# Feed-forward on one core: FP4 codes turned as packed words, scales turned and spread by DMA, remainders on GpSimd

## What is computed

```
def fp4_quant_dequant(x):                 # blocks of 16 along the last dim
    scale = max(max|x| / 6, 1e-12)
    q = GRID[searchsorted(MID, |x / scale|)] * sign(x) * scale
    # GRID = 0, .5, 1, 1.5, 2, 3, 4, 6
def fp4_linear(x, w):
    return einsum('bsk,nk->bsn', fp4_quant_dequant(x), fp4_quant_dequant(w))

x = x + attention(layernorm(x))
n = layernorm(x)                          # eps 1e-5
h = silu(fp4_linear(n, w_gate)) * fp4_linear(n, w_up)      # 512 -> 1408
out = x + fp4_linear(h, w_down)                            # 1408 -> 512
```

## Time and profile before

| | us |
|---|---|
| median of 3 runs (lowest, highest) | 3051.26 (3050.97, 3052.3) |
| the profiled execution's own time | 3052.97 |
| its span | 3051.2 |
| TensorE busy | 2989.1 (98%) |
| VectorE busy | 2622.9 (86%) |
| ScalarE busy | 1350.4 (44%) |
| GpSimd busy | 755.0 (25%) |
| DMA queue, share of 16 engines | 35.8% |
| granted TensorE clock over the run | 0.993 |

### The profile page before, as it was taken

One profiled execution on the slowest core, in us unless ns is written; L12 is line 12 of the kernel. 1 busy time (PEld: TensorE's weight loads), 2 busy tenths in 40 slices (PEclk: granted clock), 3 DMA queues, 4 the chain that ended last, 5 costly groups with the idle time before them and its releaser, 6 DMA issues.

```text
span 3051.2 us, 65181 instructions
## 1 busy us (share of the span) xinstructions
PE 2989.1 (98%) x23204; PEld 2208.6 (72%) x23204; DVE 2622.9 (86%) x4209; ACT 1350.4 (44%) x2010; POOL 755.0 (25%) x680
## 2 busy tenths in 40 slices
PE   7999899999999999889999999999999999999999
PEld 6787644444444444478888888888888888888887
DVE  7999788889889888888888888888888888888886
ACT  5666577877777787532222222222222222222221
POOL 3444200000000000023333333333333333333332
PEclk9999899999999999999999999999999999999999
DMA  7889856655655665521111111111111111101110
GB/s 244 283 289 300 275 123 143 149 133 137 154 133 138 149 137 137 151 84 32 38 42 42 42 35 35 42 41 42 42 33 36 42 42 41 42 30 40 42 35 15
DMA packets 247628, 304.20 MB, mean 100 GB/s; under 512 B 21968, under 2 KB 154960, under 8 KB 247504
## 3 DMA queue, kind: packets, MB, share of 16 engines
q1 hardware_dynamic: 247504, 302.88, 35.8%
HBM read 190.35 MB, written 112.46 MB: 99 GB/s over the span
## 4 chain that ended last, share of the span: by engine, by line
PE 56%; DVE 1%; ACT 0%; DMA 0%; issue 0%; POOL 0%; SPq 0%; DVEq 0%
PE p_ring L1845 20%; PE p_ring L1873 16%; PE ps_od L1845 11%; PE ps_od L1825 5%; PE p_ring L1863 3%; PE p_ring L1853 1%; DVE sb_wg_lo L1751 0%; PE ps_od L1873 0%; PE p_ring L1825 0%; PE p_ring L1888 0%; DVE sb_fp_tmp L102 0%; DVE sb_wd_lo L1751 0%; DMA dn<-sb_fp_tmp 0%; DVE sb_h_amax L88 0%; DVE sb_stage L1722 0%
## 5 line engine op out<-in xcount | busy, mean ns | idle before, releaser
L1040 ACT ACTIVATE sb_probs<-scores 128x1024 f32<-128x1024 f32 (+3 forms) x512 | 405.8, 840 | 113.7 <-PE scores L1246 107.3
L788 POOL TENSOR_TENSOR sb_at_in<-sb_at_in,sb_inv_in 128x512 f32<-128x512 f32 x64 | 89.0, 1390 | 1069.0 <-DMA sb_inv_in<-dinv 1068.3
L1845 PE MATMUL p_ring<-sb_wg_hi,sb_xq_hi 128*128 128x512 f32 (+1 forms) x1024 | 295.2, 369 | 0.3 <-DVE sb_wd_lo L1751 0.3
L1548 POOL TENSOR_TENSOR sb_stage<-sb_stage,sb_h_inv 128x512 f32<-128x512 f32 (+1 forms) x192 | 210.8, 1098 | 339.2 <-DVE sb_h_inv L94 339.2
L1845 PE MATMUL p_ring<-sb_wg_lo,sb_xq_hi 128*128 128x512 f32 (+1 forms) x1024 | 290.5, 365 | 0.0
L1845 PE MATMUL p_ring<-sb_wg_hi,sb_xq_lo 128*128 128x512 f32 (+1 forms) x1024 | 289.9, 364 | 0.0
L1873 PE MATMUL p_ring<-sb_wd_hi,sb_ht_hi 128*128 128x512 f32 x693 | 275.9, 398 | 0.0
L1246 PEld LDWEIGHTS scores<-sb_q_hi,sb_k_hi 32*128 32x128 f32 x1536 | 73.7, 182 | 278.3 <-ACT sb_probs L1040 154.6
L1873 PE MATMUL p_ring<-sb_wd_hi,sb_ht_lo 128*128 128x512 f32 x693 | 270.2, 390 | 0.0
L1873 PE MATMUL p_ring<-sb_wd_lo,sb_ht_hi 128*128 128x512 f32 x693 | 269.8, 389 | 0.0
L1554 POOL TENSOR_TENSOR sb_stage<-sb_stage,sb_h_scale 128x512 f32<-128x512 f32 (+1 forms) x192 | 190.0, 989 | 267.4 <-DVE sb_stage L104 267.4
(11 more groups left out here) (203 smaller groups left out, 7172.3 us busy)
## 6 DMA issues: line engine op xcount, KB each, us to landing
kq<-sb_kq_out SPq DMA_DIRECT2D x32, 1024.0 KB, 7.2
sb_kq_raw<-kq SPq DMA_DIRECT2D x64, 512.0 KB, 6.8
sb_xin<-in_L_attn_x_dram SPq DMA_DIRECT2D x32, 512.0 KB, 6.9
v<-sb_v_out SPq DMA_DIRECT2D x64, 256.0 KB, 6.5
rq<-sb_r_out SPq DMA_DIRECT2D x64, 256.0 KB, 4.4
sb_qr<-rq SPq DMA_DIRECT2D x32, 512.0 KB
sb_kr_hi<-kr SPq DMA_DIRECT2D x32, 512.0 KB
sb_kr_lo<-kr SPq DMA_DIRECT2D x32, 512.0 KB
```

What stands on the lines that cost most here:

```text
L1040: act.activation(probs(k)[:, 2 * pair:2 * pair + 2, off:BANK], scores[(2 * k + pair) % RING2][:, :, off:BANK], ACT.Exp, scale=SCALE).then_ ...
L1548: pool.tensor_tensor(x, x, spread(h_inv[:, a // QB:b // QB], (b - a) // QB), ALU.mult).then_inc(h_y, 1)
L1845: i = pe.matmul(ps[:, m, 0:b0 - a0], xt[a][:, c, :], wg[b][:, m, c, a0:b0], start=(c == 0 and a == b == 0), stop=(c == DC - 1 and a == 1))
```

## The change

What TensorE turns is no longer the quantised float32 tile. After the two rounding steps ScalarE writes the value as an unsigned byte, code = value * 2^23 + 64, four features to a 32-bit word; one 128x128 transpose of words turns 512 features. VectorE decodes out of PSUM (`decode`: byte minus 64, times the turned scale) into SBUF. The block scales are turned by themselves: VectorE's 32x32 transpose of 128x32, a DMA to a scratch tensor in DRAM, and a DMA back that spreads each row over four partitions (for slice 2 three DMAs). The product with the scale before turning (L1711 and `hidden_q`) is gone. The normalisation of x moves from VectorE (L1697) to ScalarE (`normalise`), for which GpSimd makes a shift. Both `rest_of_x` and `rest_of_hidden` move from VectorE, where they read PSUM, to GpSimd, where they read SBUF. `x_in` is gone: x is loaded straight into `x1` by its own DMA. The silu result is written into h in place. The orders of all bodies are changed, `rest_of_attention` on GpSimd and the output store on SP among them. Weight columns are turned in the order c, c+4, c+8, ... so that the packing matches.

The diff, cut to its core ("..." marks what is left out):

```
+def fp4_half_scales(dve, x, amax, scale, inv, sem, base):
+    dve.tensor_reduce(amax, blocks_of(x), AX_X, ALU.max, apply_absolute_value=True).then_inc(sem, 1)
+    own(dve, sem, base + 1)
+    dve.tensor_scalar(scale, amax, SIXTH / 2, MIN_SCALE / 2, ALU.mult, ALU.max).then_inc(sem, 1)
...
 # SyncE
             def body(b, j):
                 q, r = b * HALF + j // UNROLL3, j % UNROLL3
+                if exists(q, r + 2):
+                    sp.wait_ge(stored[(r + 2) % 4], count(q, (r + 2) // 4 * 4, 4, 16))
+                    ahead.load_x(sp, b, j + 2)
                 if exists(q, r + 3):
                     sp.wait_ge(ps_free, number(q, r, "WO") + RING3 + 1)
                     ahead.load_tile(sp, b, j + 3)
-                if exists(q, r - 1):
-                    store(b, j - 1)
+                if exists(q, r + 1):
+                    store_x_scale(q, r + 1)
+                    spread_x_scale(q, r + 1)
+                for s in range(2):
+                    spread_h_scale(q, r, s)
                 if exists(q, r + 3):
                     sp.wait_ge(ahead.at_divided, count(q, r, 1, 3))
                     ahead.load_inverse(sp, b, j + 3)
+                spread_h_scale(q, r, 2)
+                if exists(q, r - 1):
+                    store(b, j - 1)
 # GpSimd
             def inverse_deviation(q, r):
+                pool.wait_ge(ln_steps, count(q, r, 3, 2))
+                pool.tensor_tensor(negmean[:], moments[:, 0:1], minus[:], ALU.mult).then_inc(s_rstd, 1)
                 pool.wait_ge(ln_steps, count(q, r, 3, 3))
                 pool.tensor_tensor(rstd[:], vareps[:], mhalf[:], ALU.pow).then_inc(s_rstd, 1)
+                own(pool, s_rstd, count(q, r, 3, 3))
+                pool.tensor_tensor(shift[:], negmean[:], rstd[:], ALU.mult).then_inc(s_rstd, 1)
+            def rest_of_x(q, r):
+                pool.wait_ge(x_hi, count(q, r, 1, 1))
+                pool.tensor_tensor(xt_lo[:], x_values, xt_hi[:].bitcast(F32), ALU.subtract).then_inc(x_rest, 1)
+            def rest_of_hidden(q, r, j):
+                a, b = HT_CHUNKS[j]
+                pool.wait_ge(ht_rounded, count(q, r, 2, j + 1))
+                pool.tensor_tensor(ht_lo[:, a:b], values(j), ht_hi[:, a:b].bitcast(F32), ALU.subtract).then_inc(ht_rest, 1)
...
+                if exists(q, r - 1):
+                    if exists(q, r + 1):
+                        pool.wait_ge(x_chain, count(q, r + 1, X_STEPS, SCALES_STEPS + 1))
+                    rest_of_hidden(q, r - 1, 0)
+                hidden_y(q, r, 0)
+                pool.wait_ge(h_round, count(q, r, 3 * ROUND_STEPS, ROUND_STEPS))
+                if exists(q, r - 1):
+                    rest_of_hidden(q, r - 1, 1)
                 if exists(q, r + 2):
                     divide(q, r + 2)
-                hidden_y(q, r, 0)
...
+                hidden_y(q, r, 1)
+                if exists(q, r + 1):
+                    rest_of_x(q, r + 1)
+                hidden_y(q, r, 2)
                 if exists(q, r + 2):
                     rest_of_attention(q, r + 2)
-                hidden_y(q, r, 1)
-                hidden_q(q, r, 0)
-                hidden_y(q, r, 2)
-                hidden_q(q, r, 1)
-                hidden_q(q, r, 2)
 # ScalarE
+            def normalise(q, r):
+                act.wait_ge(s_rstd, count(q, r, 3, 4))
+                act.activation(xq[:], x1[:, r % 4, :], ACT.Identity, bias=shift[:], scale=rstd[:]).then_inc(x_normed, 1)
+            def code_x(q, r):
+                act.wait_ge(x_chain, count(q, r, X_STEPS, X_STEPS))
+                act.activation(x_codes[:].bitcast(U8), xq[:], ACT.Identity, bias=code_zero[:], scale=CODE_STEP).then_inc(x_coded, 1)
...
+                if following:
+                    normalise(q, r + 1)
                 if exists(q, r - 1):
                     round_hidden(q, r, 0)
...
+                magic_h(q, r, 0)
+                if following and not first:
+                    code_x(q, r + 1)
                 silu_of(q, r, 1)
-                magic_h(q, r, 0)
+                code_hidden(q, r, 0)
                 if exists(q, r + 2):
                     round_attention(q, r + 2)
                 silu_of(q, r, 2)
                 magic_h(q, r, 1)
...
                     round_x(q, r + 1, (q, r))
                 magic_h(q, r, 2)
+                code_hidden(q, r, 1)
...
+                code_hidden(q, r, 2)
 # VectorE
+            def decode(out, words, scales):
+                return dve.scalar_tensor_tensor(out=out, in0=bytes_of(words)[:, 0:out.shape[1]],
+                                                scalar=CODE_ZERO, in1=scales, op0=ALU.subtract, op1=ALU.mult)
...
+                dve.transpose(h_turned[:, s], h_scale[:, s * P // CODES:(s + 1) * P // CODES]).then_inc(h_turned_done, 1)
 # TensorE
-                for c in range(DC):
-                    i = pe.transpose(ps[:, 0, c * P:(c + 1) * P], xq[:, c * P:(c + 1) * P], ident[:])
-                i.then_inc(ps_ready, 1)
+                pe.wait_ge(x_coded, count(q, r, 1, 1))
+                pe.transpose(ps[:, 0, 0:P], x_codes[:], ident[:]).then_inc(ps_ready, 1)
...
-                pe.wait_ge(ps_free, number(q, r + 1, "HT1") + RING3 + 1)
+                pe.wait_ge(ht_rest, count(q, r, 2, 2))
```

More of the change, by code:

```diff
@@ L94, in fp4_scales @@
     dve.tensor_scalar(inv, inv, TIES, None, ALU.mult).then_inc(sem, 1)
+CODE_ZERO = 64.0
+CODE_STEP = float(2 ** 23)
+CODES = 4
+CONSTANT_BYTES = float(np.frombuffer(bytes([64] * CODES), np.float32)[0])
+def fp4_half_scales(dve, x, amax, scale, inv, sem, base):
+    dve.tensor_reduce(amax, blocks_of(x), AX_X, ALU.max, apply_absolute_value=True).then_inc(sem, 1)
+    own(dve, sem, base + 1)
+    dve.tensor_scalar(scale, amax, SIXTH / 2, MIN_SCALE / 2, ALU.mult, ALU.max).then_inc(sem, 1)
+    own(dve, sem, base + 2)
+    dve.reciprocal(inv, scale).then_inc(sem, 1)
+    own(dve, sem, base + 3)
+    dve.tensor_scalar(inv, inv, TIES / CODE_STEP, None, ALU.mult).then_inc(sem, 1)
 def fp4_round(dve, y, big, tmp, sem, base):
@@ L742, in __init__ @@
         self.in_loaded = [sem(f"in_loaded{i}") for i in range(2)]
+        self.x_loaded = [sem(f"ffn_x_loaded{i}") for i in range(2)]
         self.loads = [sem(f"prep_loaded{i}") for i in range(PREP_SLOTS + LATE_SLOTS)]
@@ L1384, in feed_forward @@
         h_round = sem("h_round")
-        h_q = sem("h_q")
+        h_coded = sem("h_coded")
         ht_rounded = sem("ht_rounded")
+        ht_rest = sem("ht_rest")
+        constants = sem("ffn_constants")
+        x_coded = sem("x_coded")
+        x_rest = sem("x_rest")
+        x_turned_done = sem("x_scale_turned")
+        x_scale_stored = sem("x_scale_stored")
+        x_spread_loaded = sem("x_spread_loaded")
+        h_turned_done = sem("h_scale_turned")
+        h_scale_stored = sem("h_scale_stored")
+        h_spread_loaded = [sem(f"h_spread_loaded{j}") for j in range(2)]
         stored = [sem(f"out_stored{i}") for i in range(4)]
@@ L1488, in _ @@
             ahead.load_chunk(sp, 2 * B - 1)
+            ahead.load_x(sp, 0, 1)
             ahead.load_tile(sp, 0, 2)
@@ L1558, in _ @@
             rest_of_attention(0, 1)
+            rest_of_x(0, 0)
             def body(q, r):
@@ L1731, in round_hidden, with decode_hidden @@
                 dve.wait_ge(h_magic, count(q, r, 3, s + 1))
[L1732 removed]
+                fp4_round(dve, h[:, a:b], h_big[:, h_slot(r, s), 0:b - a], h[:, a:b], h_round,
                           count(q, r, 3 * ROUND_STEPS, s * ROUND_STEPS))
[L1735 to L1741 removed]
+            def decode_hidden(q, r, j):
+                dve.wait_ge(h_spread_loaded[j], count(q, r - 1, (32, 48)[j], (32, 48)[j]))
+                ps = read_out(q, r, f"HT{j}")
+                if j == 0:
+                    for s in range(2):
+                        i = decode(h_values[:, CODES * s:CODES * s + CODES], ps[:, 0, s * P:s * P + P],
+                                   shared(h_spread[s]))
+                else:
+                    i = decode(rest_q, ps[:, 0, 0:P], h_spread[2])
+                i.then_inc(ps_free, 1)
             def result(q, r):
@@ L1832, in gate_up @@
                 if s == 0:
-                    pe.wait_ge(ps_free, number(q, r - 1, "XT") + RING3 + 1)
+                    pe.wait_ge(x_rest, count(q, r, 1, 1))
                 if flags(q, r)[0] and s == 2:
```

222 lines of the change are left out of this document (141 added, 81 removed).

## The result

The changed kernel takes 3185.24 us (median) against 3051.11 us before, run on the same chip: a ratio of 1.0435, 95% interval 1.0417 to 1.0452. It is slower by 134 us. (One of the changed kernel's four runs took 3285.67 us at a granted clock of 0.845; the ratio leaves it out.) The prediction said slower, by 64 us; the size is about twice what it gave, and lies above its range.

What follows compares the result with a forecast made beforehand. The prediction took TensorE to bound the kernel at 27.00 us a tile, and a loop through VectorE and GpSimd the changed one. Terms +60, +2 and +1 gave +63 on 3052.97, so 3116, median 3115; range 3045 to 3150.

Steps and rivals of the forecast that it cites:

- What TensorE saves: TensorE's transposes fall from 15 to 4: 1.03 us less a tile, 25.97 us if nothing holds it.
- The rival in which TensorE stays the bound: Feed-forward tiles stay limited by TensorE's own work at 25.97 us each: 2988 us in all, chance 0.11.
- The new lap: Loop from one WO through `residual` and `rest_of_attention` to the next WO: 27.99 us, 0.99 longer than before.
- One port: VectorE and GpSimd exclude each other when both read two SBUF inputs: 0.73 us more in the lap.
- The sum, "61 laps of +0.99: 60 us": Feed-forward tiles 2 to 63: WO waits in 62 of them, giving 61 longer laps, 60 us.
- Tile 0 to 2, with the weights: +2: Start of the run: 2 us longer, between -2 and +6, with `rest_of_attention` last there too.
- the x loads cost nothing: no wait of theirs is last: Loading x straight into place by its own DMA adds no time, since other waits end later.
- The tail, +1: End of the run: two tiles without the wait save 2 us, last steps give back 3.
- The last step, from 3116 to the median: From the profiled execution's 3116 us to the median of the runs, 1.71 lower, given as 3115.
- The codes' way: Byte codes and scales arrive in time; decode of x takes 0.69 us, the transpose of scales 0.20.

Runs made afterwards that it cites:

- e11: Changed kernel with the edits of e4, e7 and e9's move of `rest_of_x`, feed-forward loop written out instead of shifted: 2998.34 us.
- e4: Changed kernel with `rest_of_attention` moved on GpSimd ahead of `rest_of_x` instead of last: 3139.73 us.
- e9: e5 with `rest_of_x` moved from GpSimd back to VectorE, between the roundings of hidden slices 1 and 2: 3015.16 us.
- e1: Changed kernel with the feed-forward's hardware loop written out on the compute engines, SyncE keeping its own loop: 3133.1 us.
- e5: Changed kernel with 32 idle instructions ahead of VectorE's loop: 3136.95 us.
- e6: Kernel before the change with 20 idle instructions ahead of VectorE's loop, moving its start from 723 to 743: 3074.24 us.
- e7: Changed kernel with x of tile 1 loaded right behind tile 0's instead of behind all weight loads: 3175.38 us.

## Why the prediction was wrong in size

- **What TensorE saves: right.** 25.97 us a tile if nothing holds TensorE; 26.10 in `e11`. The rival in which TensorE stays the bound was priced at 2988 us, and the kernel with the holds removed takes 2998.
- **The new lap: right in order and size.** Forecast 27.99, measured 28.0 to 28.2, and 28.06 as a mean where no turn disturbs it. WO waits for `rest_of_attention`, 1.97 us of TensorE time a tile as forecast, and `e4` removed that wait and got the laps of 27.0 that follow from it.
- **One port: right, and it was the smaller part.** L1662 took 1.48 and L122 1.66 us. On the loop it cost GpSimd about what was forecast (0.73): L1662 takes 1.27 at its shortest, and the `hidden_y` 2 behind it 1.29 where the same step takes 0.85 in `e9`, together 0.65 us a lap. No run takes away the exclusion by itself. `e9` has one of the same size in its lap of 26.2 us, where TensorE is the bound again and covers it. The exclusion costs only what it delays on the loop; taking `rest_of_x` out of GpSimd's order was worth 1.9 us a lap. The three steps ahead of WO on GpSimd, and behind them the rounding of slice 2, are one queue.
- **The sum, "61 laps of +0.99: 60 us": the step that failed.** It took one lap from the middle of a group for all of them. 13 of the 61 contain a turn of the hardware loop, each 3.1 to 3.9 us longer, 45 us in all; with the lap after some turns and 0.1 us on the other laps in the loop that is 50 us in the laps. The whole run became 52 us shorter by `e1`, 48 by `e5`. Two things made them: TensorE's slack behind VectorE was gone, which the prediction had itself worked out without asking what else it had covered, and the loop had moved by 20 instructions into a bad place, which alone cost the kernel before 21 us in `e6`. The trace of the kernel before held a sign of it: laps of 27.5 and then 26.4 once in four.
- **"Tile 0 to 2, with the weights: +2": wrong.** It was +15.8. The prediction passed over the order on SP in the preparation ("the x loads cost nothing: no wait of theirs is last"). `e7` shows 10 us of it to be the late load of x, and the rest goes with `e4`'s edit on GpSimd.
- **The tail, +1: nearly right,** +3.3 by the traces.
- **The last step, from 3116 to the median:** 3116 less 1.71 is 3114, not 3115. It changes nothing.
- **The codes' way: right.** Decode 0.65 us, transposes 0.20 to 0.21, landings in time: no wait on a spread is among the long ones.

The forecast's terms of +60, +2 and +1 were measured as 63 (laps, by `e1` against the kernel before: 61 x 1.03), 16 and 3, plus 50 in the laps for the loop: 132, the difference of the two spans.

## What to carry to other kernels

When a change takes away the slack of a bound engine, list everything that slack hid, once a tile and once a loop turn, and follow a lap across the loop's boundary too. Before moving a step to an idle engine, look at what stands behind it there and who waits for that: one subtraction returned to the busier engine won 122 us. And before judging any small edit to a program with hardware loops, know that its effect may be that of the loop's place; shift it or write it out as a control.

## What was not expected of the hardware

- The cost of a loop's turn on VectorE depends on where the loop lies in the program. Places 723, 743, 759 and 775 of the first instruction gave: short pause (2.1 to 2.3 us, covered), long (4.2 to 6.7 us), none, none. By the Trainium skill, Runtime: NRT & Kernel Launch, section Instruction fetch mechanics, instructions come in blocks of 256, two are held, and a taken branch to a block that isn't held stops the engine for a fetch. The trace agrees that a turn brings a fetch: 3 to 5 packets of instructions within 8 us behind each taken branch of the changed kernel, none where it falls through. That the fetch depends on whether the loop lies within two blocks is not shown. With edges at every 256th place of the program (768, 1024) the loop that begins at 775 lies within two blocks and the one at 759 does not, yet neither has a pause; the edge that the runs show lies between 743 and 759. Why place 743 is worse than 723 (few instructions left in the first block, so that the second is wanted at once) is not tested.
- Moving VectorE's loop by 20 idle instructions changed a finished kernel by 0.7%, more than many real edits.
- A VectorE decode of bytes that lie four apart in PSUM runs at 0.65 us for 512 columns, no slower than a 512-column step on f32.
